# Scores of even heads from the lower row half and of odd heads from the upper one, and V's product one score later

## What is computed

```python
q = _split(lora_linear(x, Wq, bq, Bq, Aq))      # 16 heads of 16 features
k = _split(lora_linear(x, Wk, bk, Bk, Ak))
v = _split(lora_linear(x, Wv, bv, Bv, Av))
scores = jnp.einsum('bhqd,bhkd->bhqk', q, k) * SCALE
attn = jax.nn.softmax(scores, axis=-1)
out = jnp.einsum('bhqk,bhkd->bhqd', attn, v)
return lora_linear(out, Wo, bo, Bo, Ao)
```

## Time and profile before

| what | value |
|---|---|
| median of 3 runs | 415.2 us (414.1 to 416.36) |
| the profiled execution's own time | 415.58 us |
| its span, first to last instruction | 413.4 us |
| TensorE matmul busy | 366.8 us (89%) |
| VectorE busy | 308.2 us (75%) |
| ScalarE busy | 249.9 us (60%) |
| mean granted TensorE clock | 0.955 of full speed |

### The profile page before, as it was taken

The page is one execution under the profiler, slowest core; times in us unless marked ns, Lnnn a source line. Parts: engine busy times, 40 slices in busy tenths (PEclk is TensorE's granted clock), DMA queues, the critical chain, the costliest instruction groups (busy, mean ns, idle before and its releaser), DMA issues.

```text
span 413.4 us, 6021 instructions
## 1 busy us (share of the span) xinstructions
PE 366.8 (89%) x2157; PEld 167.5 (41%) x2157; DVE 308.2 (75%) x501; ACT 249.9 (60%) x433; POOL 150.4 (36%) x169
## 2 busy tenths in 40 slices
PE   7998889989999999989989997988889598977696
PEld 4544421212221222222123435775665365544485
DVE  7469987988888887978852354685898879999543
ACT  2672137888888898888989665233443363562331
POOL 4050189960000000000000013354877768947143
PEclk9999957999999999999999999999899789899799
DMA  7768723534000000000000000000000000000001
GB/s 195 252 116 132 186 39 61 106 70 88 2 0 2 0 2 0 2 0 2 1 1 2 2 0 0 2 2 0 2 1 2 0 0 2 25 1 2 25 2 51
DMA packets 14672, 14.22 MB, mean 34 GB/s; under 512 B 5235, under 2 KB 12979, under 8 KB 14454
## 3 DMA queue, kind: packets, MB, share of 16 engines
q1 hardware_dynamic: 12214, 11.70, 12.6%
q10 hardware_dynamic: 2176, 1.64, 1.3%
q0 software_dynamic: 256, 0.52, 0.8%
HBM read 5.40 MB, written 1.06 MB: 16 GB/s over the span
## 4 chain that ended last, share of the span: by engine, by line
PE 58%; DVE 21%; ACT 13%; issue 4%; DMA 1%; POOL 1%; ACTq 1%; DVEq 0%
PE ps L1354 16%; PE ps L1340 11%; ACT pbuf L869 10%; PE ps L1494 6%; PE ps L1483 4%; DVE mx L1051 4%; PE ps L1317 4%; DVE s_wide L1152 4%; PE ps L1269 3%; DVE xn L980 3%; PE ps L1468 3%; DVE pack L1141 2%; PE ps L1529 2%; DVE stats L963 2%; PE ps L1258 1%
## 5 line engine op out<-in xcount | busy, mean ns | idle before, releaser
L869 ACT ACTIVATE pbuf<-ps,exp_scale 128x512 f32<-128x512 f32 x256 | 158.3, 691 | 31.5 <-PE ps L1340 31.1
L1051 DVE TENSOR_REDUCE mx<-ps 128x1 f32<-128x1024 f32 x128 | 150.9, 1220 | 24.9 <-PE ps L1317 24.3
L1340 PE MATMUL ps<-pack 64*128 64x512 f16 x256 | 88.8, 391 | 7.8 <-ACT pbuf L869 1.3
L1354 PE MATMUL ps<-pbuf,v_slot 128*32 128x512 f32 x512 | 69.1, 611 | 5.1 <-ACT parts L854 3.2
L1340 PEld LDWEIGHTS ps<-pack 64*128 64x128 f16 x256 | 19.9, 94 | 97.3 <-issue 52.6
L1317 PE MATMUL ps<-pack 64*128 64x512 f16 x128 | 50.1, 395 | 4.6 <-DVE mx L1051 4.2
L1494 PE MATMUL ps<-w_nat,pack 128*128 128x256 bf16 x384 | 52.3, 280 | 1.7 <-POOL pack L719 1.6
L731 POOL TENSOR_TENSOR pbuf<-wT 128x1024 f32<-128x1024 f32 (+3 forms) x32 | 49.9, 1573 | 8.5 <-ACT wT L920 8.5
L1317 PE MATMUL ps<-parts,pack 64*128 64x512 f16 x128 | 51.2, 404 | 0.0
L694 POOL COPY v_slot<-v_sb 128x512 f32<-128x512 f32 x8 | 4.9, 613 | 127.3 <-PE ps L1354 105.9
L719 POOL TENSOR_TENSOR pack<-pack 128x256 bf16<-128x256 f32 x64 | 42.1, 668 | 24.7 <-DVE pack L1141 24.7
(11 more groups left out here) (136 smaller groups left out, 393.8 us busy)
## 6 DMA issues: line engine op xcount, KB each, us to landing
w_nat<-in_L_ffn_w_dram SPq DMA_DIRECT2D x2, 1024.0 KB, 8.2
pack<-pack SPq DMA_DIRECT2D x3, 512.0 KB, 4.8
pack<-pbuf SPq DMA_DIRECT2D x20, 64.0 KB, 2.8
x_res<-in_L_attn_a_x_dram SPq DMA_DIRECT2D x4, 256.0 KB, 3.7
pack<-parts SPq DMA_DIRECT2D x16, 64.0 KB, 2.3
pack<-parts SPq DMA_DIRECT2D x32, 32.0 KB, 2.0
out_dram<-x_res SPq DMA_DIRECT2D x4, 256.0 KB, 2.1
w_nat<-in_L_attn_b_Wqkv_dram ACTq DMA_DIRECT2D x1, 768.0 KB, 5.2
```

The source lines that it names most:

```text
L869: act.activation(pbuf[:, c % 2, j, :], ps[:, b, :], ACT.Exp, scale=exp_scale[:, 0:1]).then_inc(drained[b], 1)
L1051: dve.tensor_reduce(mx[:, par, k:k + 1], ps[:, b:b + 2, :].rearrange("p b k -> p (b k)"), AX_X, ALU.max) \
L1340: pe.matmul(ps[:, b, :], k_group[0:ROWS, at, j, P * c:P * c + P].rearrange("p g t -> p (g t)"), q_rows[0:ROWS, at, qh, j, :].rearrange("p ...
L1354: ins = pe.matmul(ps[32 * j:32 * j + 32, PV_BANK, :], v_slot[:, qh, c, j, :], pbuf[:, c % 2, j, :], start=(c == 0), stop=(c == TT - 1))
```

## The change

1. Keys of every head lie in both row halves. `k_far` is gone; the far keys go to the upper rows of `k_rows`. Group 0 gets one more copy (64 rows x 4 heads x 512 keys) from lower to upper rows, and the key copies of groups 1 to 3 double, from 64x4x512 to 64x4096.
2. `score_tile` takes rows 64 to 127 for odd heads, rows 0 to 63 for even ones.
3. `land_shift` issues two DMAs, one for each row half, and the waits count to 32 for each shift.
4. Three scores are done ahead of the loop rather than two; s runs from 3 to 34, and block c's product stands behind s = 4c+6.

```diff
@@ last_unit_slots
-    for s in range(2, STEPS):
+    for s in range(3, STEPS):
         yield LAST_STEP * s, ("score", s)
@@ far_keys
-            spread(eng, k_far[ROWS:2 * ROWS, h, :], K_, h, slice(HALF, T), done)
+            spread(eng, k_rows[ROWS:2 * ROWS, h, HALF:T], K_, h, slice(HALF, T), done)
@@ sync engine, behind the copy of group 0's second query half
+            for j in range(G):
+                sp.wait_ge(head_packed[j], 32)
+            sp.dma_start(k_rows[ROWS:2 * ROWS, 0:G, 0:HALF], k_rows[0:ROWS, 0:G, 0:HALF]).then_inc(far_keys_packed, 16)
@@ whole_group
-                sp.dma_start(k_far[ROWS:2 * ROWS, G * g:G * g + G, :], k_rows[0:ROWS, G * g:G * g + G, HALF:T]) \
-                    .then_inc(group_repeated[g], 16)
+                sp.dma_start(k_rows[ROWS:2 * ROWS, G * g:G * g + G, :].rearrange("p h t -> p (h t)"),
+                             k_rows[0:ROWS, G * g:G * g + G, :].rearrange("p h t -> p (h t)")).then_inc(group_repeated[g], 16)
@@ land_shift
-                sp.dma_start(q_rows[SHIFT_ROWS[g // 2], g, qh, :, :].rearrange("o h t -> o (h t)"),
-                             m_rows[0:TWO * n, :]).then_inc(shift_landed, 16)
+                rows = SHIFT_ROWS[g // 2]
+                for r in (0, ROWS):
+                    sp.dma_start(q_rows[rows.start + r:rows.stop + r:rows.step, g, qh, :, :].rearrange("o h t -> o (h t)"),
+                                 m_rows[0:TWO * n, :]).then_inc(shift_landed, 16)
@@ scalar engine, ahead of the first exponential
-            for done in (far_keys_packed, second_half_packed):
-                act.wait_ge(done, 16 * G)
+            act.wait_ge(far_keys_packed, 16 * G + 16)
+            act.wait_ge(second_half_packed, 16 * G)
@@ score_tile
-                pe.matmul(ps[:, b, :], k_group[0:ROWS, at, j, P * c:P * c + P].rearrange("p g t -> p (g t)"),
-                          q_rows[0:ROWS, at, qh, j, :].rearrange("p g t -> p (g t)"), start=True, stop=True) \
+                r = slice(ROWS * (j % 2), ROWS * (j % 2) + ROWS)
+                pe.matmul(ps[:, b, :], k_group[r, at, j, P * c:P * c + P].rearrange("p g t -> p (g t)"),
+                          q_rows[r, at, qh, j, :].rearrange("p g t -> p (g t)"), start=True, stop=True) \
                     .then_inc(filled[b], 1)
@@ tensor engine, ahead of the loop
-                if k == LEAD - 3:
-                    pe.wait_ge(far_keys_packed, 16 * G)
-                    pe.wait_ge(shift_landed, 16)
-                if k >= LEAD - 3 and k < LEAD - 1:
-                    score_tile(0, 0, 0, k - (LEAD - 3))
+                if k == LEAD - 4:
+                    pe.wait_ge(far_keys_packed, 16 * G + 16)
+                    pe.wait_ge(shift_landed, 32)
+                if k >= LEAD - 4 and k < LEAD - 1:
+                    score_tile(0, 0, 0, k - (LEAD - 4))
@@ unit
-                for s in range(2, STEPS + 2):
+                for s in range(3, STEPS + 3):
...
-                            pe.wait_ge(shift_landed, (u + 2) * 16)
+                            pe.wait_ge(shift_landed, (u + 2) * 32)
...
-                    if s % G == 1 and s > G:
+                    if s % G == 2 and s > G:
                         times_v(qh, u, s // G - 1)
```

More of the change, by code:

```diff
@@ L322, in build @@
         last_halves = parts[:, 2048:8192].bitcast(F16).rearrange("p (m a t) -> p m a t", m=2, a=TWO + 1)
-        k_far = parts[:, 8192:16384].bitcast(F16).rearrange("p (h t) -> p h t", h=H)
         o_un = parts[:, 0:8192].bitcast(F32).rearrange("p (g t) -> p g t", g=NG)
@@ L329, in build @@
         k_group = pack[:, 0:16384].bitcast(F16).rearrange("p (g j t) -> p g j t", g=NG, j=G)
-        far_group = parts[:, 8192:16384].bitcast(F16).rearrange("p (g j t) -> p g j t", g=NG, j=G)
         g_full = pack[:, 0:12288].bitcast(F32).rearrange("p (k f t) -> p k f t", k=KEPT, f=FC)
@@ L1314, in max_tile @@
                     pe.wait_ge(drained[b], base[b] + u * (FILLS // 2) + k // 2)
-                for n, keys in ((0, k_group[0:ROWS, at, j, 0:HALF]), (1, far_group[ROWS:2 * ROWS, at, j, :])):
+                for n, keys in ((0, k_group[0:ROWS, at, j, 0:HALF]), (1, k_group[ROWS:2 * ROWS, at, j, HALF:T])):
                     q = q_rows[ROWS * n:ROWS * n + ROWS, at, qh, j, P * qt:P * qt + P]
```

## The result

| | before | changed |
|---|---|---|
| median of the runs | 414.65 us (413.4 to 416.36) | 401.56 us (400.32 to 406.14, 4 runs) |
| ratio | | 0.9702, 95% interval 0.9615 to 0.9788 |
| profiled execution: time, span | 415.58, 413.4 us | 402.37, 400.2 us |
| its granted clock, mean | 0.955 | 0.949 |

13.1 us less where 16.0 were forecast: faster, inside the range, and 2.4 us above the number.

What follows compares the result with a forecast made beforehand. The loop was taken as bound by a chain of product, exponential and score, not one engine, and unit 7 by TensorE. -11.8 - 2.1 - 2.2 - 1.3 + 0.3 + 1.0 = -16.1 took 415.58 to 399.5 us (median 399.2), range 393 to 406.

Steps and rivals of the forecast that it cites:

- the late shift of unit 1: Unit 1's shift lands behind group 2's copies on the same queue, keeping TensorE waiting: +1.0 us, range 0 to 2.5.
- the late shift of unit 2: Unit 2's shift behind group 3's copies, with 1 us more room: nothing, at most 1.5 us.
- units 1 to 5, without it: Five full loop units, each 2.35 us shorter (0.21 + 6 x 0.26 + 0.58): -11.8 us.
- unit 7, its row-half slots: In unit 7, bound by TensorE, six pairs or triples of scores each save a 0.21 us slot: -1.3 us.
- The loop: Product behind the third score: chunk 1.00 + 0.42 + 0.69 + 0.05 + 0.32 = 2.48 us instead of 2.74.
- Rival 1: In the loop, the score's passage is hidden and ScalarE binds: units about 19.1 us, total 391.5; 7%.
- The start: Before the loop: later shift and extra score cost 0.8, an earlier second product returns 0.5: +0.3 us, bounds -0.5 to +1.5.
- Rival 2: At the start and the shifts of units 1 and 2, queued copies cost 4.2 us more: 403.5 us; 12%.
- Rival 3: The loop gains half, as the shift's room or a maximum tile waiting for VectorE holds TensorE: chunks 2.60, 406 us; 11%.
- the 0.12 of room: In the shift's chunk, 0.12 us left between `cut_max` and the transposition: costed at nothing, 0.2 a unit for the range.
- Rivals 4 and 5: 4, the loop: another wait replaces the removed one, 415 us, 4%; 5, the loop: clock stays low, 417 to 425, 5%.
- Rival 5: Loop: TensorE's clock stays at 1.2 GHz after mostly paired maximum tiles; 13 to 20 chunks low, 417 to 425 us; 5%.

Runs made afterwards that it cites:

- e1_product_only: The kernel before with only the product moved behind the third score, nothing of the row halves; 399.98 us, ratio 0.9635.
- e2_halves_only: The changed kernel with the product back behind the second score; row halves, doubled key copies and two shift DMAs stay; 414.22 us, ratio 0.9958.
- e8_maxima_ahead_of_product: e4_copies_behind_shift with maximum tiles behind even s instead of odd, so one stands between third score and product; 408.54 us, ratio 0.9829.
- e1_again: e1_product_only run again unchanged, beside another group of kernels; 400.55 us, ratio 0.9661.
- e4_copies_behind_shift: The changed kernel with the key copies of groups 2 and 3 issued behind the shifts of units 1 and 2; 398.39 us, ratio 0.9565.
- e5_behind_fourth_score: e4_copies_behind_shift with the product one score later, behind the fourth score; 426.84 us, ratio 1.0306.

## Why the prediction was right, and where it was off

The difference between the two profiled executions, cut at the starts of the units (first products), beside the terms of the forecast:

| | forecast | measured |
|---|---|---|
| up to unit 1, without the late shift | -2.1 + 0.3 | -3.2 |
| the late shift of unit 1 | +1.0 | +0.9 |
| the late shift of unit 2 | 0 | +3.4 |
| units 1 to 5, without it | -11.8 | -11.7 |
| unit 6 | -2.2 | -2.1 |
| unit 7, its row-half slots | -1.3 | -0.9 |
| behind unit 7 | 0 | +0.4 |
| sum | -16.1 | -13.2 |

Unit 1's start moved from 86.95 to 84.59, -2.36, of which +0.87 is the late shift: its chunk was 3.28 instead of 2.48 and the hand-over 2.80 instead of 2.73. For unit 2's shift it is 5.07 instead of 2.48 (99.71 to 104.78), 3.35 instead of 2.73, and 2.75 instead of 2.55 in the next unit's first chunk. The last two, 0.8 together, have no idle time in them: they are the clock.

**The loop: right, by its own mechanism.** Every term of the chunk's sum stands in the timeline with its size. `e1_product_only` and `e2_halves_only` show that it is the product's place and not the halves. `e8_maxima_ahead_of_product` moves one term by 0.21 and the chunk follows by 0.21.

**Rival 1, ScalarE as the bound: no.** The score's passage of 0.32 isn't hidden. Its other reading was the rule of up to 2x cited from the Trainium skill (TensorEngine Tiling (Array Packing), Theoretical Speedup). `e2_halves_only` has the pairs, and its chunk stays 2.74. In unit 7 the halves gave 0.91 of 25.70 us. The trace bears out the sum by path, not the rule as a price of the whole.

**Unit 7: right in kind, 0.4 too high.** Six pairs or triples were priced at one slot each. Comparing chunk by chunk with `e1_product_only` (3.27, 3.46, 4.24, 4.25, 3.48, 4.51, 2.48 there; 3.06, 3.24, 4.03, 4.03, 3.44, 4.51, 2.48 here), four gave 0.21, the fifth 0.04 and the sixth nothing. Behind the sixth TensorE waits for ScalarE, 0.35 us in the one kernel and 0.56 in the other: the slot that was saved went into that wait. I had read the unit as TensorE's throughout.

**The start: below its lower bound here, mostly by luck.** It was priced at +0.3 with -0.5 as its lower bound, and came out at about -1.1 in this execution. The step said that the later shift and one more score at the low clock cost 0.8, and that an exponential step gives back 0.5. The second product came at 65.77, 1.26 ahead of the 67.03 of the earlier trace rows. TensorE did wait at the first score, 1.39 us until 57.16. The window from 62 to 67 us, of the changed kernel:

```profile
62.00:67.00 5.00, 4.87 (x30) 0.89 (x28) 3.71 (x4) 3.59 (x7) 4.72 (x4) 0.76 0.30 57
```

and of the kernel before:

```profile
62.00:67.00 5.00, 5.00 (x19) 0.88 (x16) 3.00 (x3) 3.00 (x5) 4.72 (x4) 0.52 0.32 58
```

The granted clock there is 0.76 instead of 0.52. I had carried the lower level through the first chunk; here it was left earlier. The change is not shown to be the reason, since executions of one kernel differ by as much. The changed kernel's second profile has 0.53 in that window and its second product at 66.56; unit 1 starts at 84.73 without a wait for its shift, which leaves -0.1 for the start. `e1_product_only` and `e1_again`, one kernel, have 0.77 and 0.60, and second products at 65.66 and 66.78. `e4_copies_behind_shift` waited the same 1.39 us and has 0.54. So what the wait costs, and when the clock comes back, these runs do not settle, and some 1 us of this row is luck, which hid about a third of the loss at the shifts.

**The late shifts: here the forecast failed.** The copies' landing was sized rightly: 6.9 us behind the first issue was forecast, group 3's landed at 6.8 (103.6 - 96.85), and the shifts at 7.15 and 7.18. The cited rule of the Trainium skill (DMA: Bandwidth & Descriptors, Queues, rings and completion order), by which each DMA engine takes the descriptors of one queue in ring order, agrees as far as it goes; it fixes the order of taking and not of finishing, and the finishing is the trace's. The second copy, issued at 97.41, has 6.2 us to landing in its line's view, 103.6, and the shift issued behind it landed at about 104.0. It overtook nothing. The step that failed is "Group 3 repeats this with 1 us more room: nothing", with 1.5 as its bound, where 3.4 were measured. Against this 1 us more, it had 1.8 us less. Two things were missing in that step. The issue of the shift's DMAs is itself held up behind the copies, 4.03 us instead of 1.51, and the next layout with its 16.28 us comes after it. And the unit that has to cover the queue's cycle had just become 2.35 shorter, which stood in the same working. And a third, smaller one: the clock fell behind the idle time, 0.8 beyond the wait itself (1.1 in the changed kernel's second profile, with 3.81 for the hand-over instead of 2.73). `e4_copies_behind_shift` closes the account: without these waits the kernel is 4.1 faster, against the 0.9 + 3.4 of the table.

**Rival 2, the queue of copies costs more**, had this mechanism and 4.2 us for it, of which 1.2 at the start. It came true for the shifts, by 3.3, and not at the start, which went the other way by 1.4 in the profiled execution; hence a result between the forecast and this rival. **Rival 3:** `cut_max` held the transposition only in unit 0, where the chunk was 2.82 instead of 2.65; from unit 1 on it was 2.64, so the 0.12 of room was enough. **Rivals 4 and 5:** products are not 2.74 apart, and the clock is 1.00 in the undisturbed units. Behind the start, the one stretch of low clock in the loop is that behind the late shift. Rival 5 also misread what TensorE did ahead of its low clock: from 36 to 48 us maximum tiles were not most of it, but some 3.5 us beside 6.8 us of other products (L1287).

## What to carry to other kernels

A loop in which three engines are 85 to 93% busy can have slack on all of them. Its period is a closed chain, and it is worth summing start to start before an engine is blamed; what gets off that chain is worth its full length, and what is made faster beside it (the paired scores) nothing. A stage that becomes shorter covers less: every transfer that had room in it has to be costed again against the new length, with the issue on its queue as part of the cycle. A small, urgent DMA goes ahead of large ones that aren't needed yet.

## What the runs showed of the hardware

- The issue of a small DMA behind 1 MB of copies on its queue: two of 8 KB took 3.0 to 4.0 us on SyncE instead of 1.4 to 1.5, and ended 5.22 to 5.23 us behind the first copy's issue in every row of the table, whenever they began.
- After 2.72 us without a matmul inside a loop at full clock, the granted clock averaged 0.66 in the window from 105 to 110 us, and 0.8 us went beyond the wait itself. After 1.60 us it stayed at 1.00 in units 1 to 5 of `e5_behind_fourth_score` and fell to 0.61 and 0.50 in its unit 6.
- At the loop's start the clock comes back at different times in executions of one kernel: 0.76 and 0.53 from 62 to 67 us in the changed kernel, 0.77 and 0.60 in `e1_product_only` and `e1_again`.
- A matmul in the upper rows starts ahead of ones in the lower rows that stand before it in the queue. In the kernel before the maximum tile's upper one, fourth behind the product, starts at 127.24, and the second and third at 127.45 and 127.67.
- An exponential started 0.42 us behind the start of its score in most orders, and 0.50 in the two kernels with the product behind the fourth. What makes the 0.08 is open.
